# Two-part graph network on one core: a small product of zeros behind each releasing product of the convolutions

## The reference, cut to what matters

```
deg  = segment_sum(1, dst) (with loops);  dinv = rsqrt(deg);  norm = dinv[src] * dinv[dst]
def conv(x, W, b):
    h = x @ W
    return segment_sum(h[src] * norm, dst) + b          # loops included
for W, b, a, g, beta in three layers (width 256):
    h = elu(layernorm(conv(h, W, b) * sigmoid(a)) * g + beta)
out = conv(h, W3, b3)                                   # width 128
x = layernorm(x + out)
# then two attention layers over the same edges, and a last layernorm
```

## Time and profile before

| | |
|---|---|
| executions | 7992.43, 8002.68, 8004.82 us |
| profiled execution | 7992.59 us, span 7990.8 us |
| mean granted clock of TensorE | 0.776 of full speed |
| busy PE, DVE, POOL, ACT | 64%, 48%, 42%, 8% of the span |
| L1850 (gathered tiles) | 4800 records |
| L1832 (dense tiles) | 3920 records |
| convolutions | about 835 to 4490 us |

### The profile page before, as it was taken

The page is one execution under the profiler, slowest core; times in us unless marked ns, Lnnn a source line. Parts: engine busy times, 40 slices in busy tenths (PEclk is TensorE's granted clock), DMA queues, the critical chain, the costliest instruction groups (busy, mean ns, idle before and its releaser), DMA issues.

```text
span 7990.8 us, 113877 instructions
## 1 busy us (share of the span) xinstructions
PE 5148.4 (64%) x25539; PEld 3913.9 (49%) x25540; DVE 3862.7 (48%) x10619; ACT 675.7 (8%) x1598; POOL 3354.1 (42%) x3512
## 2 busy tenths in 40 slices
PE   2677566665777667775556565666676555666666
PEld 1121445554565556664445444545555444555555
DVE  8544356542333323343334455555555455555555
ACT  0011000000000000000000100111111100011111
POOL 0000555445444444444554455444433355544441
PEclk9755666767888888897777777788888777787777
DMA  1011322323333333333222233333222233332321
GB/s 42 32 52 76 95 75 76 92 84 94 103 101 108 100 90 103 97 89 95 74 79 90 79 113 107 99 96 92 88 84 76 77 109 104 103 97 89 86 84 50
DMA packets 308013, 695.45 MB, mean 87 GB/s; under 512 B 68843, under 2 KB 118116, under 8 KB 306526
## 3 DMA queue, kind: packets, MB, share of 16 engines
q0 software_dynamic: 146944, 381.90, 16.9%
q10 hardware_dynamic: 94612, 196.31, 7.4%
q1 hardware_dynamic: 66250, 114.82, 4.8%
HBM read 624.93 MB, written 67.83 MB: 87 GB/s over the span
## 4 chain that ended last, share of the span: by engine, by line
PE 31%; DVE 23%; another core or an unknown queue 18%; issue 14%; DVEq 10%; ACT 2%; DMA 1%; ACTq 0%; SPq 0%; POOLq 0%; POOL 0%
PE acc_ps L1832 7%; PE acc_ps L1850 7%; PE acc_ps L1784 3%; PE q_ps L1774 3%; DVE dots L993 2%; DVE wide L990 2%; DVE masks L788 2%; DVE masks L808 2%; DVE even_rows L582 1%; PE q_ps L1755 1%; PE bank L1886 1%; DVEq L466 1%; DVEq L788 1%; DVEq L459 1%
## 5 line engine op out<-in xcount | busy, mean ns | idle before, releaser
L1388 POOL DMA_INDIRECT ring<-rows,idx_stage x3360 | 3318.3, 988 | 3177.4 <-DVEq L838 1010.6
L1850 PE MATMUL acc_ps<-ring,masks 128*128 x4800 | 1198.7, 413 | 820.3 <-DVE masks L788 741.9
L1850 PEld LDWEIGHTS acc_ps<-ring,masks 128*128 128x128 f32 x4800 | 966.0, 250 | 1027.7 <-issue 937.6
L1774 PE MATMUL q_ps<-odd_rows,conv_only 128*128 (+1 forms) x3904 | 766.9, 366 | 943.9 <-DVE conv_only L796 767.5
L788 DVE SCALAR_TENSOR_TENSOR masks<-dst_f,neg_first,lane 128x256 f32<-128x256 f32 x1200 | 542.8, 483 | 1331.3 <-remote 624.1
L1774 PEld LDWEIGHTS q_ps<-odd_rows,conv_only 128*128 128x128 f32 x3904 | 685.4, 267 | 1007.5 <-issue 1003.3
L1784 PE MATMUL acc_ps<-msg,masks 128*128 x3904 | 661.9, 322 | 323.3 <-DVE msg L1005 299.7
L1784 PEld LDWEIGHTS acc_ps<-msg,masks 128*128 128x128 f32 x3904 | 611.0, 227 | 444.9 <-issue 433.7
L808 DVE SCALAR_TENSOR_TENSOR masks<-dst_f,neg_first,lane 128x512 f32<-128x512 f32 x488 | 366.8, 752 | 572.3 <-remote 394.1
L1376 POOL COPY idx_stage<-src_idx 128x28 int32 (+1 forms) x126 | 29.6, 235 | 1355.9 <-DVE turn_b L729 810.5
L1755 PE MATMUL q_ps<-bias_rows,zeros_bf 128*128 128x512 bf16 x1450 | 456.5, 456 | 0.0
(11 more groups left out here) (278 smaller groups left out, 6264.9 us busy)
## 6 DMA issues: line engine op xcount, KB each, us to landing
conv_only<-dst_rows SPq DMA_DIRECT2D x394, 256.0 KB
ring<-rows,idx_stage POOLq DMA_INDIRECT x3360
adjacency<-odd_rows ACTq DMA_DIRECT2D x10, 3136.0 KB, 8.9
conv_only<-adjacency ACTq DMA_DIRECT2D x70, 384.0 KB
msg<-adjacency ACTq DMA_DIRECT2D x60, 384.0 KB
wide<-adjacency ACTq DMA_DIRECT2D x60, 384.0 KB
turn_b<-adjacency ACTq DMA_DIRECT2D x60, 384.0 KB
part<-adjacency ACTq DMA_DIRECT2D x30, 448.0 KB
```

The lines of the kernel that those rows point to most:

```text
L1388: pool.indirect_dma_start(ring[:, j, 0:WIDTH[p]], None, tables[p][:, :], bass.IndirectOffsetOnAxis(ap=idx_stage[:, half, j:j + 1], axis=0) ...
L1774: ins = pe.matmul(to, mask_t[:, u, j, :], q_rows[:, bass.ds(t + u, 1), :].rearrange("p a f -> p (a f)"), start=u == 0, stop=u == nxt)
L1850: ins = pe.matmul(to, masks[:, u, j, :], rhs, start=False, stop=final and j == GC - 1)
```

## The change

A new helper `add_zeros` issues one bf16 product: weights `zeros_bf` (128x128 zeros), moving operand 64 columns of the same array, accumulated onto the first 64 columns of the tile's sum. It adds nothing to any semaphore and waits for none. It is called behind each A-part of a dense tile but the last (after the product that adds to `parts_used`), and behind each group of a gathered tile but the last (after the second of the two products that add to `masks_used`). The sums keep their values.

```diff
--- before.py
+++ after.py
@@ -1817,6 +1817,10 @@
                 if final:
                     add_group(p, t, last, True, 0)
 
+            def add_zeros(to):
+
+                return pe.matmul(to[:, 0:64], zeros_bf[:, :], zeros_bf[:, 0:64], start=False, stop=False)
+
             def own_row(p, t, to):
 
                 F = WIDTH[p]
@@ -1832,6 +1836,8 @@
                         ins = pe.matmul(to, parts(p)[q % PART_RING][:, r * P:(r + 1) * P], rows_in[p][:, k, 0:WIDTH[p]],
                                         start=False, stop=k == TILES - 1)
                     ins.then_inc(parts_used, 1)
+                    if q < len(PARTS) - 1:
+                        add_zeros(to)
 
             def conv_edges(p, t, at, to):
 
@@ -1849,6 +1855,8 @@
                             rhs = ring[:, bass.ds(slot + j, 1), 0:F].rearrange("p a f -> p (a f)")
                             ins = pe.matmul(to, masks[:, u, j, :], rhs, start=False, stop=final and j == GC - 1)
                         ins.then_inc(masks_used, 1)
+                    if not final:
+                        add_zeros(to)
 
                 group(first, False, 1)
                 with pe.Fori(first + 1, last) as g:
```

## The result

The changed kernel took 8040.78 us, the median of seven runs (8029.2 to 8047.5). The kernel before, run beside it on the same chip, took 8004.82 us (seven runs, 7992.4 to 8023.9). The ratio is 1.0041, with a 95% interval of 1.0027 to 1.0054. So it is slower, by 36 us, where 8055 was forecast.

What follows compares the result with a forecast made beforehand. A chain that changes engines, with a ring of products, masks and gathers, was taken to bound the kernel. Dense 41 plus gathered 17 = 58 us on 7992.6 gave 8050.6, predicted 8055; own range 8020 to 8100, eight in ten 7955 to 8140.

Steps and rivals of the forecast that it cites:

- The price of one: TensorE: a lone small bf16 product among fp32 ones costs 0.11 us at 2.4 GHz, 0.19 at 1.2.
- The upper bound of 0.33: TensorE: highest price of one product, 0.33 us, read from an existing bf16 product with 3 rows.
- The dense term: Dense tiles: all 280 products count, with no wait to hide them, 280 x 0.145 = 41 us.
- the mean price of 0.145: Convolutions: price per product in us, averaged over 56% of the time at 2.4 GHz and the rest at 1.2.
- The gathered term: Gathered tiles: 245 of 444 products stand in a stream, 47% of their cost on the chain, 17 us.
- Releases: Mask releases from TensorE to VectorE: a following product does not bring them out sooner, so no gain is credited.
- the 60 us that were named: VectorE's remote wait ahead of the masks, near 624 us in 77: moving over 60 us makes the forecast wrong.
- C: Rival, late stretches: followers bring releases out sooner, kernel gets faster, 7950 with 13 waits gone, 7850 with a third; chance 0.21.
- D: Rival, late stretches: added records make more of them, nine more add 73 us, 8130; chance 0.15.
- Its sign: New line's records on TensorE: gaps above 0.3 us behind them at 2.4 GHz decide for more late stretches.
- B: Rival, gathers on POOL set the pace and hide the price: 0 to 16 us stay, 8010; chance 0.14.
- The sum: Whole kernel: 41 + 17 = 58 us on the profiled execution's 7992.6, so 8050.6; predicted 8055.

Runs made afterwards that it cites:

- dense_five: Kernel before plus five products of zeros behind each dense A-part but the last (280 places), none in gathered tiles: 6798.42 us, ratio 1.005 to the kernel before.
- after_again: The changed kernel, unchanged, run again on another, faster chip beside the kernel before: 6782.28 us, ratio 1.0031.
- each_half: The changed kernel plus 600 products of zeros, one between the two halves of every gathered group: 6801.41 us, ratio 1.0058 to the kernel before.
- before_again: The kernel before, unchanged, run again on another, faster chip: 6759.69 us, ratio 0.9996.

## Why the prediction was right

The price of a product, the direction and the cause were right. The terms of the sum were less so: the dense one was 41 us against 28, and the gathered one agrees with its measurement by luck.

**The price of one: right.** 0.11 us at 2.4 GHz was forecast and 0.11 measured: 2.70 against 2.59 us for a part, and five times over in `dense_five`. At 1.2 GHz 0.19 was forecast. In the changed kernel there, TensorE's timeline, where the granted clock is 0.50 (the third number from the end of the first line, a row of a stretch):

```profile
858.00:860.60 2.60, 2.60 (x14) 2.60 (x13) 0.00 (x0) 0.00 (x0) 0.00 (x0) 0.50 0.73 234
...
857.89 0.26 PE L1822 MATMUL acc_ps<-zeros_bf 128*128 128x64 bf16 x1
857.97 2.91 PE L1836 MATMUL acc_ps<-even_rows,msg 128*128 128x128 f32 x12
860.67 0.26 PE L1822 MATMUL acc_ps<-zeros_bf 128*128 128x64 bf16 x1
```

857.89 to 857.97 is 0.07 (0.072 unrounded), and the twelve records from 857.97 to 860.67 take 2.70 us, against 12 x 0.213 = 2.56 by the pitch that the forecast used: 0.07 + 0.14 = 0.21 us. The upper bound of 0.33, from the product of 3 rows, had no part in it.

**The dense term: mis-sized, 41 us, measured 28.** Two steps of it failed. The first is the mean price of 0.145, taken from the clock of the whole convolutions (0.78). In the dense tiles 256 of the 280 products run where the granted clock is 1.00, 24 where it is 0.50, so the price there was 256 x 0.11 + 24 x 0.21 = 33 us in all. The second step said "there is no wait in which the small product could hide", from one tile of a 256-wide convolution. For the 128-wide ones that was wrong: their records take half the time, the parts then come no faster than they are loaded, and the cost of 140 of the 280 products nearly disappears in that. On the first chip the 128-wide pairs went from 352 to 355 us and the 256-wide ones from 505 to 530. Of these 25 us, 15 are the price: 130 of the 140 products there cost 0.11 us each. At the other ten a longer pause follows, but in before 8 of the 140 places where one part follows another had such a pause as well. What adds the remaining 10 us I can't tell apart from the scatter of the late stretches.

**The gathered term: 17 us, measured 18, by a wrong count.** The step took 444 - 199 = 245 products as exposed. In the changed kernel only 150 of the 444 have the next record within 0.1 us behind them, 37 within 0.1 to 0.3, and 257 stand ahead of a longer wait. That would give 150 x 0.145 x 0.47 = 10 us. The 18 us are the difference of two single executions, and the three estimates of this half that I have are 4 us (ratio 1.0005, not different from nothing), 18 (one profile against another) and 18 with an uncertainty of 15. Between 0 and 18 is what is shown, so the agreement of 17 with 18 is luck.

**Releases: right.** "I give the follower no credit": the remote wait ahead of the masks went from 624.1 us in 77 waits to 663.3 in 89, inside the 60 us that were named, and late or unrecorded releases from 428 to 441; on the third chip, from 495 to 481. C is refuted for this kernel: where releases are late a follower mends nothing. D's size, 8130, did not come either. Its sign, a gap above 0.3 us behind the new record at 2.4 GHz, does not decide: there are 183 such gaps in the changed kernel and 190 in `after_again`, where one release at most is late, so they are waits for masks and parts that were there anyway. Ahead of the new records TensorE waited for an issue 12 times, 11.1 us in all:

```profile
L1822 PE MATMUL acc_ps<-zeros_bf x724: 192/193/261, 838.4 to 4532.6; 128*128 128x64 bf16 x181
its engine sat idle before it (us, times) until:
  issue: 11.1, 12
```

**B, hidden by the gathers: not as the whole answer, in part open.** B's 8010 missed the measured 8041, and the 19 us of `each_half` over the change speak against a full cover. On the chips without late stretches the gathers hold 10% of the chain, and the change costs 20 us instead of 36. The corrected terms there are 140 x 0.11 = 15 us for the 256-wide dense tiles, 0 to 9 for the 128-wide, and, with 121 exposed products in `after_again`, 121 x 0.11 x 0.47 = 6 for the gathered ones: 21 to 30. Measured are 20, with an interval from 13 to 30, so it is not shown that anything more is given back there. The test that should have separated B failed, so how much of the gathered term is covered by the gathers and how much by the masks stays open.

**The sum.** 58 us were forecast; 48 were measured between the profiled executions and 36 between medians. The forecast of 8055 lies 14 us above the measured time, though the loss itself was put 22 too high: the 58 were laid on the low profiled execution (7992.6), and on the median now measured beside the change (8004.8) they would give 8063. That these two errors stand against each other is luck.

## What to carry to other kernels

A product that computes nothing is not free even where TensorE is idle a third of the time: in a stream of fp32 records a single short bf16 one costs 0.11 us, while the next four beside it cost 0.03 each. Count such insertions by where they stand: in the unbroken stream of a tile they cost in full, ahead of a wait of the same engine little or nothing (2.10 us a group with and without). Ahead of a release, or in the middle of a group, they came out dearer than behind the release, but far below the full price. And read the waits of every size of tile before you say that a stream has none: one width filled TensorE, the other waited for its loads. And take the clock of the stage in which the insertion stands: 0.78 was the mean, and the dense tiles ran nearly all at 1.00.

## What the runs showed of the hardware

The same program took 8004.82 us beside the changed kernel, and 6760.67, 6762.25 and 7986.68 in the three sets of runs, on three different chips. In the profiles of the two slower sets VectorE stands idle up to 18.1 us ahead of L788 with no sender found, and of the 1200 releases of one line 428 and 495 are late or unrecorded in the kernels without the product; in the eight profiles of the two faster sets there is one such or none. The records of semaphores show it for TensorE's releases; some of the 428 may only lack their record, since 1015 of the 1200 have one in before and all have one in `before_again`. What makes a chip do this was not settled; a kernel that is compared must run beside its base on the same chip.

An indirect gather of 16 rows holds POOL 0.85 us, one of 128 rows 0.95.
